# Turning softmax probabilities with VectorE, through a DRAM round trip, instead of with TensorE

## The reference

```
q = x @ wq.T; k = concat(ctx, x @ wk.T); v = concat(ctx, x @ wv.T)
attn = softmax(q @ k.T * scale)          # 512 x 1024 per batch
x = x + tanh(g) * (attn @ v) @ wo.T
x = x + tanh(g2) * moe(layernorm(x))     # 16 experts, top 4, plus a shared MLP
```

## Time and profile before

| | |
|---|---|
| median of 3 runs | 1162.15 us (1158.1 to 1165.61) |
| profiled execution | 1167.74 us |
| its span, first to last instruction | 1166.1 us |
| granted clock of TensorE, mean | 0.96 |
| PE busy | 1045.0 us (90%) |
| DVE busy | 659.1 us (57%) |
| ACT busy | 394.3 us (34%) |
| POOL busy | 506.8 us (43%) |

### The profile page before, as it was taken

How to read it: one execution, slowest core, us unless ns; L and a number is a source line. 1 busy time by engine, 2 the same in 40 slices (tenths; PEclk the granted TensorE clock), 3 DMA queues, 4 the chain that set the end, 5 groups by cost and what they waited for, 6 DMA issues and landing times.

```text
span 1166.1 us, 18150 instructions
## 1 busy us (share of the span) xinstructions
PE 1045.0 (90%) x4995; PEld 886.3 (76%) x4996; DVE 659.1 (57%) x1125; ACT 394.3 (34%) x652; POOL 506.8 (43%) x546
## 2 busy tenths in 40 slices
PE   6999999999999999948888989889888878887888
PEld 5888878878888778847777878778787777776565
DVE  4444574484364599645555645545565655546657
ACT  4421321231132224124444444444444444432112
POOL 6412020211203330556566656656665756625751
PEclk9999999999999999969899989999999999998988
DMA  8053663491455561347776766666666666657863
GB/s 325 2 145 145 212 185 114 123 300 72 110 205 210 195 225 59 136 127 203 211 207 200 210 195 193 209 203 205 202 209 196 211 200 197 206 166 270 252 206 120
DMA packets 128638, 214.55 MB, mean 184 GB/s; under 512 B 50720, under 2 KB 80544, under 8 KB 125344
## 3 DMA queue, kind: packets, MB, share of 16 engines
q1 hardware_dynamic: 101568, 145.58, 39.9%
q0 software_dynamic: 16672, 49.70, 14.4%
q10 hardware_dynamic: 10368, 18.88, 4.5%
HBM read 163.25 MB, written 63.44 MB: 194 GB/s over the span
## 4 chain that ended last, share of the span: by engine, by line
PE 65%; DVE 11%; issue 9%; another core or an unknown queue 5%; ACT 4%; DVEq 2%; DMA 1%; ACTq 1%; SPq 1%; POOL 0%
PE ps_products L89 20%; PE c_ps_u L89 13%; PE c_ps_y L89 10%; PE ps_scores L89 7%; PE b_ps_u L89 5%; PE d_ps_u L89 3%; PE b_ps_y L1041 2%; DVE expert_lo L1688 1%; DVEq L1536 1%; PE d_ps_y L1041 1%; PE ps_transposed L717 1%; DVE xT_lo L1668 1%; DVE hT_lo L1683 1%; DVE d_ps_t L1900 1%
## 5 line engine op out<-in xcount | busy, mean ns | idle before, releaser
L1500 POOL DMA_INDIRECT xs<-xn_dram,column x288 | 300.8, 1044 | 91.9 <-issue 89.7
L89 PE MATMUL c_ps_u<-expert_hi,xT_hi 128*128 x576 | 189.5, 329 | 8.7 <-issue 8.7
L89 PE MATMUL c_ps_u<-expert_lo,xT_hi 128*128 x576 | 188.2, 327 | 1.5 <-issue 1.3
L89 PE MATMUL c_ps_u<-expert_hi,xT_lo 128*128 x576 | 188.0, 326 | 1.4 <-issue 1.4
L89 PE MATMUL c_ps_y<-expert_hi,hT_hi 128*128 (+1 forms) x216 | 95.5, 442 | 73.9 <-DVE hT_lo L1683 54.8
L89 PEld LDWEIGHTS c_ps_u<-expert_hi,xT_hi 128*128 128x128 f32 x576 | 111.2, 193 | 15.1 <-issue 11.4
L1688 DVE TENSOR_TENSOR expert_lo<-stage,expert_hi 128x1088 f32 x72 | 93.4, 1297 | 44.0 <-issue 43.3
L89 PEld LDWEIGHTS c_ps_u<-expert_lo,xT_hi 128*128 128x128 f32 x576 | 111.1, 193 | 4.7 <-issue 1.5
L89 PEld LDWEIGHTS c_ps_y<-expert_hi,hT_hi 128*128 128x128 f32 (+1 forms) x216 | 43.9, 203 | 92.8 <-issue 85.8
L89 PEld LDWEIGHTS c_ps_u<-expert_hi,xT_lo 128*128 128x128 f32 x576 | 111.0, 193 | 1.2 <-issue 1.2
L76 POOL TENSOR_TENSOR idle<-idle 128x1 f32<-128x1 f32 x76 | 25.4, 334 | 191.5 <-DVE column L1661 107.9
(11 more groups left out here) (299 smaller groups left out, 2338.4 us busy)
## 6 DMA issues: line engine op xcount, KB each, us to landing
stage<-we SPq DMA_DIRECT2D x76, 544.0 KB
y_dram<-y ACTq DMA_DIRECT2D x72, 256.0 KB
h_dram<-hf SPq DMA_DIRECT2D x72, 192.0 KB
hs<-h_dram SPq DMA_DIRECT2D x72, 192.0 KB
xs<-xn_dram,column POOLq DMA_INDIRECT x288
ctxT_raw<-ctxT SPq DMA_DIRECT2D x4, 1024.0 KB, 6.6
ctx_raw<-ctx SPq DMA_DIRECT2D x4, 1024.0 KB, 4.9
r_t<-x SPq DMA_DIRECT2D x4, 1024.0 KB, 5.3
```

Of the source, the lines that this page charges most:

```text
L89: last = pe.matmul(out, a[i], b[j], start=(n == 0), stop=(n == 3 * len(pairs) - 1))
L1500: pool.indirect_dma_start(xs[:, g, :], None, rows, bass.IndirectOffsetOnAxis(ap=sources[:, g:g + 1], axis=0)).then_inc(sem, 16)
```

## The change

Of the four row tiles of a batch, the first three are no longer turned by PE (`TRIPS = IT - 1`). ACT stores `prob` to a DRAM buffer (512 KB, in pieces of 512 bytes), waits for it, and loads it back into `p_rows` so that each partition holds four rows (pieces of 2 KB). DVE turns it in blocks of 32x32 into `p_turned` (two instructions of 128x512 per row tile), ACT makes `pT_hi` from `p_turned` and DVE `pT_lo`; both read `p_turned` with a distance of 128 bytes from one element to the next. The fourth row tile is turned by PE as before, and its exponential is made in two instructions. `p_rows` and `p_turned` lie in the place of `r_t`, so that the load of `r_t` and the `spare` copy move behind the last split. The new keys are stored in block order, so the key order of the softmax columns changes, and the context rows are laid out to fit on the host.

```
-        def exps(i):
+        def exps(b, i):
             act.wait_ge(bias_ready, nexp.up())
+            if i:
+                act.wait_ge(p_out, trip(b, i - 1))
+            else:
+                act.wait_ge(t_ready, t.now)
+            if i < TRIPS:
+                act.activation(prob[:], ps_s[:, i % 2, :], ACT.Exp, ...)
+            else:
+                for h in range(2):
+                    last = act.activation(in_chunks(prob[:, h * S:(h + 1) * S]), to_sides(ps_s[...]), ACT.Exp, ...)
+                last.then_inc(p_ready, 1)
+        def store_p(i):
+            act.wait_ge(p_ready, nexp.now)
+            act.dma_start(p_d[i % 2], prob[:].rearrange("p (g c) -> p g c", c=P)).then_inc(p_out, 16)
+        def load_p(b, i):
+            if i:
+                act.wait_ge(turned, nth(b, IT + 2 * i))
+            act.dma_start(p_rows[:].rearrange("p h b c -> p h (b c)"), p_by_side[i % 2]).then_inc(p_in, 16)
+        def high_p(b, i):
+            for h in range(2):
+                act.wait_ge(turned, nth(b, IT + 2 * i + h + 1))
+                act.activation(by_four(pT_hi[:, 4 * h:4 * h + 4, i * P:(i + 1) * P]), turned_rows(h), ACT.Copy).then_inc(turned_hi, 1)
...
# ACT, behind the q and k halves of a batch
+            exps(b, 0)
+            store_p(0)
+            exps(b, 1)
+            load_p(b, 0)
+            store_p(1)
+            exps(b, 2)
+            load_p(b, 1)
+            store_p(2)
+            high_p(b, 0)
+            if b is not None:
+                router(b)
+            exps(b, 3)
+            load_p(b, 2)
+            high_p(b, 1)
+            high_m(k_hi[:, 0, :])
+            high_m(k_hi[:, 1, :])
+            high_p(b, 2)
+            high_m(k_hi[:, 2, :])
             trans(IT - 1)
             high_m(k_hi[:, IT - 1, :])
...
# DVE
+        def turn_p(b, i):
+            dve.wait_ge(p_in, trip(b, i))
+            for h in range(2):
+                if i or b is not None:
+                    dve.wait_ge(turned_split, nth(b, IT + 2 * i - 1 + h))
+                dve.transpose(p_turned[:, 4 * h:4 * h + 4, :].rearrange("p k (b r) -> p b k r", r=SIDE),
+                              p_rows[:, h, :, :].rearrange("p b (k c) -> p b k c", c=SIDE)).then_inc(turned, 1)
+        def split_p(b, i):
+            for h in range(2):
+                ...
+                dve.wait_ge(turned_hi, nth(b, IT + 2 * i + h + 1))
+                dve.tensor_tensor(by_four(pT_lo[o]), turned_rows(h), by_four(pT_hi[o]), ALU.subtract).then_inc(turned_split, 1)
...
             logits()
-            trans(0)
             if ahead:
                 next_sums(b)
             maxima(2)
+            turn_p(b, 0)
             shifted()
-            trans(1)
+            split_p(b, 0)
             if ahead:
                 next_apply(b)
             maxima(3)
+            turn_p(b, 1)
             softmax()
+            low_m(k_hi[:, 0, :], k_lo[:, 0, :])
+            split_p(b, 1)
+            turn_p(b, 2)
+            low_m(k_hi[:, 1, :], k_lo[:, 1, :])
+            split_p(b, 2)
             larger_()
-            trans(2)
-            for i, other in enumerate((equal_, added, nothing)):
-                low_m(k_hi[:, i, :], k_lo[:, i, :])
-                other()
+            low_m(k_hi[:, 2, :], k_lo[:, 2, :])
+            equal_()
             trans(IT - 1)
+            added()
             low_m(k_hi[:, IT - 1, :], k_lo[:, IT - 1, :])
...
# PE
+            pe.wait_ge(turned_split, nth(b, IT + 2 * TRIPS))      # ahead of values
-                turn(i - 1)                                        # behind S1, S2, S3
...
# SP
+        def next_r(b):
+            sp.wait_ge(turned_split, nth(b, IT + 2 * TRIPS))
+            sp.dma_start(r_t[:], x_d[b]).then_inc(res_in, 16)
+            if b:
+                sp.dma_start(spare_d[b - 1], io["x"]).then_inc(spare_in, 16)
```

More of the change, by code:

```diff
@@ L37 @@
 SIDE = 32
+TRIPS = IT - 1
 EPS = 1e-5
@@ L166, in attention_phase @@
     x_t = sb("x_t", [P, IT, D], F32)
+    over = Sbuf(nc, sb.at)
+    p_rows, p_turned = over("prob_rows", [P, 2, QUAD, P], F32), over("prob_turned", [P, KC, P], F32)
     r_t = sb("r_t", [P, IT, D], F32)
@@ L239, in attention_phase, with trip, by_four, turned_rows @@
     gate_ready, step = sem("gate_ready"), sem("dve_step")
+    def trip(b, i):
+        return (0 if b is None else b) * TRIPS * 16 + 16 * (i + 1)
+    def by_four(rows):
+        return rows.rearrange("p k (r b) -> p k r b", b=QUAD)
+    def turned_rows(h):
+        return p_turned[:, 4 * h:4 * h + 4, :].rearrange("p k (b r) -> p k r b", r=SIDE)
     def sync(sp):
@@ L389, in scalar, with high_m @@
         m, t, nexp = Count(), Count(), Count()
-        def high_m(out):
+        def high_m(out, view=lambda rows: rows):
             act.wait_ge(m_ready, m.up())
-            act.activation(out, ps_m[:, (m.n - 1) % 2, :], ACT.Copy).then_inc(m_hi, 1)
+            act.activation(out, view(ps_m[:, (m.n - 1) % 2, :]), ACT.Copy).then_inc(m_hi, 1)
         def high_t(out):
@@ L435, in attend @@
             for j in range(2 * DC):
-                high_m((q_hi if j < DC else k_hi)[:, j % DC, :])
+                high_m(q_hi[:, j, :]) if j < DC else high_m(to_sides(k_hi[:, j - DC, :]), in_chunks)
                 if b is None:
@@ L445, in attend @@
                     o = (slice(None), slice(None), slice(i * P, (i + 1) * P))
-                    act.wait_ge(r_turned, b * 4 + (i - 3))
-                    act.activation(xn2T_hi[o], xn2T[o], ACT.Copy).then_inc(r_hi_made, 1)
-            exps(0)
-            for i in range(1, IT):
-                trans(i - 1)
-                exps(i)
-                if i == 2 and b is not None:
-                    router(b)
-            for i in range(IT - 1):
-                high_m(k_hi[:, i, :])
+                    act.wait_ge(turned, nth(b, i + 1))
+                    act.activation(xn2T_hi[o], xn2T[o], ACT.Copy).then_inc(turned_hi, 1)
+            exps(b, 0)
[16 more added lines that the diff above has]
+            high_m(k_hi[:, 2, :])
             trans(IT - 1)
@@ L636, in attend @@
             for j in range(2 * DC):
-                hi, lo = (q_hi, q_lo) if j < DC else (k_hi, k_lo)
-                low_m(hi[:, j % DC, :], lo[:, j % DC, :])
+                if j < DC:
+                    low_m(q_hi[:, j, :], q_lo[:, j, :])
+                else:
+                    low_m(to_sides(k_hi[:, j - DC, :]), to_sides(k_lo[:, j - DC, :]), in_chunks)
                 if b is not None:
@@ L686, in vector @@
             k = b - 1
-            for cnt, per in ((m, 22), (t, 8), (s, 4), (steps, 20), (hm, 16), (ht, 8)):
+            for cnt, per in ((m, 22), (t, 2), (s, 4), (steps, 21), (hm, 16), (ht, 2)):
                 cnt.enter(k, per)
@@ L793, in attend @@
                 pe.wait_ge(ctx_ready, b)
-                values()
+                values(b - 1)
                 project()
@@ L850, in tensor @@
         pe.wait_ge(ctx_ready, B)
-        values()
+        values(B - 1)
         project()
@@ L1809, in load @@
             if before and tile >= 2 * IT:
-                sp.wait_ge(total_in[k], 16)
+                sp.wait_ge(own_in, IT * 16)
             elif before:
                 sp.wait_ge(other_out[k - IT], 16)
-            sp.dma_start(rows(tile)[:], (x2_d if tile >= 2 * IT else base_d)[tile]).then_inc(total_in[k], 16)
+            sp.dma_start(rows(tile)[:], (x2_d if tile >= 2 * IT else base_d)[tile]
+                         ).then_inc(own_in if k < IT else other_in[k - IT], 16)
         def store(tile):
@@ L1876, in lift @@
             k, before = place(order[c])
-            act.wait_ge(total_in[k], before * 16 + 16)
+            if k < IT:
+                act.wait_ge(own_in, (before + 1) * IT * 16)
+            else:
+                act.wait_ge(other_in[k - IT], before * 16 + 16)
             if c >= 2:
```

57 lines of the change are left out of this document (34 added, 23 removed).

## The result

| | before | after |
|---|---|---|
| median of the runs, us | 1163.88 (4 runs) | 1213.3 (1210.95 to 1221.53, 4 runs) |
| ratio to before | | 1.042, 95% interval 1.037 to 1.048 |
| profiled execution, its span, us | 1167.74, 1166.1 | 1210.95, 1209.3 |

The forecast was 1185, the range 1165 to 1197. The side was right and the size was not: 49 us lost by the medians, 43.2 by the two spans, against 22.6.

A forecast was written before the change was run, and what follows sets the result against it. PE bounds attention, but DVE's list from S3 to the values and a late third load would delay it: 17.8 us later values plus 4.8 us clock, 22.6 on 1162.15, gives 1184.8, said as 1185; range 1165 to 1197.

The forecast's parts named there:

- values later, batches 0 to 3: Attention, end of S1 to values: values start later by 3.7, 5.4, 5.8 and 2.9 us, sum 17.8.
- clock behind the values' pauses, batches 1 to 3: PE behind pauses of 5 us before the values: lower clock loses 3 x 1.6 = 4.8 us, ends 0 and 9.
- what costs nothing: Key order, host layout, `k_hi` views, later `r_t` and `spare`, the exponential's extra sum of 0.2 us: no cost.
- S3 to values decides: The stretch from end of S3 to values, where DVE is as full as PE, decides what the change is worth.
- DVE's count: DVE's work behind S3 after the change: 14.8 us, against 11.8 us for PE.
- DVE's count alone: Rival 2: trips in time, no stride surcharge or clock loss, only DVE's work counts: about +5 us, 1167; chance 0.24.
- Term (a), the surcharge: Splits and copies reading `p_turned` at 128-byte steps: 0.17 us more per instruction on DVE and ACT, ends 0 and 0.33.
- Term (c), the third load: Third load, issued as SP and POOL start 3 MB for the next batch: 6.5 us, ends 3.2 and 9.7.
- The store at 4.3: Store of 512 KB in 512-byte pieces to DRAM: 4.3 us, ends 3 and 5.
- 3 (dear steps, 1196): Rival: strides on `p_turned` cost 0.62 us per instruction, 29.5 + 4.8 us, 1196; chance 0.08.
- 4 (late load, 1194): Rival: the third load takes 9.7 us in batches 0 to 2, +3 x 3.2 us, 1194; chance 0.06.
- 1: Rival: not slower, PE stays the bound as DVE's list keeps up, -10.6 and -0.9 us, 1151; chance 0.04.

The follow-up runs named there:

- keys: The kernel before, all tiles still turned by PE, with the new key order, host layout of `ctx` and exponentials in two halves; ratio to before 1.000.
- no_trip_contiguous: The changed kernel without store and load of the tiles and without 128-byte steps in copies and splits; ratio to before 1.021 (2 runs).
- refilled: The changed kernel with reordered DVE and ACT lists, next layer norm kept early, last `spare` copy behind the shared weights' loads; ratio to before 1.029.
- ctx_late_contiguous: The refilled kernel with `ctxT_raw` and `ctxT_hi` loaded behind the third tile's split, and copies and splits without steps; ratio to before 0.997.
- spare_last: The changed kernel with the last batch's `spare` copy issued behind the loads of the shared expert's weights; ratio to before 1.031.

## Why the prediction was right on the side and wrong on the size

The sum of the prediction, term by term, against the marks (us):

| term | forecast | measured |
|---|---|---|
| values later, batches 0 to 3 | 3.7 + 5.4 + 5.8 + 2.9 = 17.8 | 6.7 + 10.3 + 10.9 + 4.8 = 32.7 |
| clock behind the values' pauses, batches 1 to 3 | 4.8 | 2.7 + 1.8 + 2.7 = 7.2 |
| tail ("what costs nothing"): wait for `r_t`, and the clock behind it | 0 | 2.8 + 1.6 = 4.4 |
| sum | 22.6 | 44.3 of 44.4 |

The steps that failed are thus the sizes in the first row, by 14.9 us (steps, the late load, POOL beside DVE, V2 at half clock), and the tail, put at nothing, by 4.4.

- **What decides.** "S3 to values decides" was right for most of it, and so was the order of events. S3 of batch 1 ended 1.7 us earlier, for 1.9 forecast. Of the waits listed, V2's and the values' came, and V3's 1.5 us for `k_lo` did not show in batch 1 (in batch 2 it was 1.49): V2 at half clock took its place. The key order at nothing was right (keys).
- **DVE's count.** 14.8 against 11.8 was the right comparison, and 14.8 the right count: no_trip_contiguous has 15.1. But the price of "DVE's count alone" (batch 1 +1.7) was wrong, for there it is +4.8: DVE waits 2.1 us for `k_hi`, and 1.2 are POOL beside it. A list passed between two engines costs its hand-overs besides its count. That the lists are a cause is shown by refilled (39.6 to 34.1, the transfers as early as in after).
- **Term (a), the surcharge.** 0.17 us taken, 0.33 the upper end, 0.42 (DVE) and 0.51 (ACT) measured. The earlier trace rows had steps of 64 bytes on one of two inputs; here it is 128 bytes, on one of the split's two inputs and on the copy's only one, and no output steps. Whether the length of the step makes the difference was not tried. By the prediction's own slope (26 us per us of surcharge) 0.42 adds 6.5 to the 17.8; with all else mended the steps are worth 7.3 (ctx_late_contiguous).
- **Term (c), the third load.** 6.5 taken, 8.1 measured in batch 1. The store at 4.3 was exact. That is within the ends given. What was missing is where else it acts: in the refilled kernel the collision, with POOL's split that moves with it, costs 22.6 us, and a store can be hit as well as a load.
- **A term left out: POOL beside DVE.** A later third split falls under POOL's `ctxT_lo`: 3.21, 3.33 and 3.10 in batches 0 to 2 instead of 2.1, 1.0 to 1.2 each.
- **The clock.** I had 4.8 for three pauses of the values; they cost 2.7, 1.8 and, in batch 3, 2.7. Left out was V2: behind its own wait of 4.3 it ran at half clock and lost 5.17 - 2.73 = 2.4 us, in the very stretch whose delay I was adding up. In batch 1 that delays V3, beside DVE's chain, which ends later. DVE's chain has the 4.9 us by which the values missed the forecast (10.3 against 5.4): the load was issued 1.2 us later than forecast (166.02 is 19.5 behind S1, against 158.0 or 18.3; the first split and its copies, 2.2 each instead of 1.6, make that) and took 1.6 longer, POOL made 1.2, the third split's steps 0.5; 0.4 is left.
- **"What costs nothing".** This failed at the tail: PE waits 3.17 us for `r_t` where it waited 0.37, and loses 1.6 at half clock behind that. I had looked for who needs the shared weights (PE at 390) and not for who works beside the engine that splits them. Before, POOL's split (369.1 to 383.8) already lay beside DVE's scale steps and one of them took 1.47. After, with the weights late (26.1 instead of 9.9), three instructions on DVE's way to `r_t` are slow: the last `b_xT_lo` (1.89 instead of 0.69), the exponential's extra sum (1.64, costed at 0.2 "beside the values"), and the scaling (1.39). In spare_last the first and the third are at 0.69 and 0.23, and the wait is 0.83. The remaining 2.7 us of the tail are the clock behind the values of batch 3, which the sum had, at 1.6, in its own term.
- **Rivals.** 3 (dear steps, 1196) and 4 (late load, 1194) were each given as the exception, and both came true in part: the surcharge was 0.42 for the 0.62 of rival 3, the load 8.1 for the 9.7 of rival 4. POOL beside DVE, V2's clock and the tail were in no rival. 1 and 2 fell.
- **The two rules cited.** The rule on 16-byte lines in the Trainium skill, SBUF — State Buffer (Door 1: The DMA port swizzle), has the right direction; the page gives no figure, and 0.42 and 0.51 us were measured. It was under-weighed. The rule on shared engines in the Trainium skill, DMA: Bandwidth & Descriptors (Issuing engines are not separate DMA queues), agrees with refilled, where a store issued from ACT took 14.3 us beside SP's and POOL's transfers.

## What to carry to other kernels

When work leaves the bounding engine for a chain of others, write the chain down with its hand-overs, and count how many units it can carry before it waits: here two tiles of four gain, and three lost in every list tried that kept its steps and trips. Undo suspected causes in pairs as well as alone, since a cause that ends 1 us earlier than another measures as zero. And of what is "hidden", ask which engine works beside it, not only who needs its result.
